# Layer 1's causal masks: from TensorE matmuls to VectorE and GpSimd

## The reference

```
# layer 1's attention; x is the modulated layer norm, 2048 x 128
k = x @ Wk
v = x @ Wv
q = jnp.einsum('btc,qcd->bqtd', x, Wq)
wei = jnp.einsum('bqtd,bsd->bqts', q, k) * scale
causal = jnp.tril(jnp.ones((t, t), dtype=bool))
wei = jnp.where(causal, wei, -jnp.inf)
wei = jax.nn.softmax(wei, axis=-1)
out = jnp.einsum('bqts,bsd->btqd', wei, v)
out = out.reshape(b, t, -1)
return out @ Wp + bp
# around it
h = _layernorm(x, axis=-1) * (1 + ca) + sa
x = x + ga * _L1_attn_ref(h, Wk, Wv, Wq, Wp, bp)
h = _layernorm(x, axis=-1) * (1 + cb) + sb
x = x + gb * _L1_ffn_ref(h, W_r, W_k, W_v, mu_r, mu_k)
```

## Time and profile before

| | us |
|---|---|
| median of three runs | 1150.22 |
| lowest, highest run | 1148.53, 1151.46 |
| profiled execution | 1151.61 |
| its span, first to last instruction | 1149.2 |
| PE busy (matmuls) | 1021.7 |
| DVE busy | 903.9 |
| ACT busy | 814.9 |
| POOL busy | 149.0 |

### The profile page before, as it was taken

How to read it: one execution, slowest core, us unless ns; L and a number is a source line. 1 busy time by engine, 2 the same in 40 slices (tenths; PEclk the granted TensorE clock), 3 DMA queues, 4 the chain that set the end, 5 groups by cost and what they waited for, 6 DMA issues and landing times.

```text
span 1149.2 us, 22131 instructions
## 1 busy us (share of the span) xinstructions
PE 1021.7 (89%) x8766; PEld 349.2 (30%) x8766; DVE 903.9 (79%) x1154; ACT 814.9 (71%) x1556; POOL 149.0 (13%) x264
## 2 busy tenths in 40 slices
PE   4658999999999999999998999899978888798895
PEld 1212222222222222222232444343434443233323
DVE  5897999998999989999988777666766568587602
ACT  3105999998999998999976676567743555466683
POOL 2005000004000013000034000410121003000100
PEclk8658999999999999999999999999989999899997
DMA  4650400002000001000003431052003211200000
GB/s 105 128 98 17 137 2 2 2 2 44 1 2 2 2 21 23 2 1 3 2 2 116 122 87 31 27 93 49 1 1 111 74 57 28 38 10 2 10 1 9
DMA packets 47259, 42.04 MB, mean 37 GB/s; under 512 B 6102, under 2 KB 45366, under 8 KB 47158
## 3 DMA queue, kind: packets, MB, share of 16 engines
q1 hardware_dynamic: 44902, 35.27, 13.2%
q0 software_dynamic: 1824, 5.25, 1.6%
q10 hardware_dynamic: 432, 0.13, 0.0%
HBM read 26.83 MB, written 13.30 MB: 35 GB/s over the span
## 4 chain that ended last, share of the span: by engine, by line
PE 65%; DVE 21%; ACT 7%; issue 3%; DMA 2%; POOL 1%; SPq 1%; POOLq 0%; DVEq 0%; ACTq 0%
PE O L875 23%; DVE mx L1120 13%; PE T L846 12%; PE S L805 7%; PE S L812 4%; ACT PT L1351 3%; PE T L855 3%; PE S L961 2%; PE S L919 1%; PE S L929 1%; PE T L969 1%; PE S L920 1%; PE S L855 1%; PE T L884 1%; DVE Vf L1180 1%
## 5 line engine op out<-in xcount | busy, mean ns | idle before, releaser
L1120 DVE TENSOR_REDUCE mx<-S 128x2 f32<-128x1024 f32 (+2 forms) x672 | 757.0, 1179 | 89.2 <-PE S L812 38.2
L1351 ACT ACTIVATE PT<-T 128x512 f32<-128x512 f32 (+2 forms) x1280 | 675.8, 581 | 118.1 <-PE T L846 46.8
L875 PE MATMUL O<-PT,Va 128*9 128x256 f32 (+1 forms) x4040 | 319.0, 388 | 3.3 <-ACT Os L1358 3.3
L805 PE MATMUL S<-Ks,Qs 48*128 48x512 bf16 x1024 | 208.0, 397 | 26.3 <-DVE mx L1120 22.0
L846 PE MATMUL T<-Qs,Ks 51*128 51x512 bf16 x1024 | 202.1, 387 | 15.3 <-ACT PT L1351 7.2
L846 PEld LDWEIGHTS T<-Qs,Ks 51*128 51x128 bf16 x1024 | 55.6, 93 | 226.4 <-issue 131.9
L875 PEld LDWEIGHTS O<-PT,Va 128*9 128x9 f32 x4040 | 60.0, 88 | 207.4 <-issue 198.0
L812 PE MATMUL S<-K,Qs 96*128 96x512 bf16 (+3 forms) x320 | 85.5, 358 | 15.7 <-DMA Qs<-rows_q 5.4
L855 PE MATMUL T<-Qs,K 99*128 99x512 bf16 (+3 forms) x256 | 72.2, 350 | 7.7 <-ACT PT L1351 4.0
L875 PE MATMUL O<-PT,V 128*17 128x512 f32 (+3 forms) x640 | 75.0, 541 | 0.0
L805 PEld LDWEIGHTS S<-Ks,Qs 48*128 48x128 bf16 x1024 | 52.5, 95 | 53.4 <-DVE mx L1120 47.9
(11 more groups left out here) (225 smaller groups left out, 835.3 us busy)
## 6 DMA issues: line engine op xcount, KB each, us to landing
Qs<-in_L_ffn_experts SPq DMA_DIRECT2D x28, 192.0 KB, 2.7
Ks<-in_L_ffn_experts SPq DMA_DIRECT2D x20, 192.0 KB, 2.6
Qs<-rows_q SPq DMA_DIRECT2D x48, 64.0 KB
Vf<-sorted_x SPq DMA_DIRECT2D x12, 256.0 KB, 4.5
sorted_y<-Vf SPq DMA_DIRECT2D x12, 256.0 KB, 2.3
Qs<-rows_q SPq DMA_DIRECT2D x24, 128.0 KB, 4.6
rows_q<-q SPq DMA_DIRECT2D x7, 384.0 KB, 2.6
sorted_x<-XP POOLq DMA_DIRECT2D x1, 1792.0 KB, 10.8
```

The lines of the kernel that those rows point to most:

```text
L805: m = e.matmul(two[:, i, :], Qs[r0:r0 + 48, hp, q0:q0 + 128], Ks[r0:r0 + 48, hp, CH * kb:CH * kb + CH], start=True, stop=True, tile_positi ...
L875: m = e.matmul(Ob[32 * g:32 * g + d1, lo:hi], v, PT[(2 * j + g // 2) % 4][:, p0 + lo:p0 + hi], start=(kt == 0 and halves[0] == 0), stop=Tr ...
L1120: e.tensor_reduce(mx[:, u % 2, h0:h0 + 2, kb], two[:, :, 0:n], AX.X, ALU.max).then_inc(free, 1)
L1351: e.activation(PT[(2 * j + pair) % 4][:, CH * i + lo:CH * i + CH], bank[:, lo:CH], ACT.Exp).then_inc(free, 1)
```

## The change

The mask matmuls of both passes are gone from PE (256 of them), and so is the tensor `mk`. In the score pass DVE does the work for diagonal tiles: instead of one reduction over both heads it issues a fused operation for each head. It adds `mq`, now 512 columns wide (zeros, and the triangle in the last 128), to the scores, writes the sum back in place to PSUM, and gives the maximum into `mx`. In the exponential pass nothing is masked before the exponential; afterwards POOL sets the entries of `PT` above the diagonal to zero, with one selection for each head pair on 128 by 2 by 128 elements, and signals `masked`. PE's PV waits for that signal in these steps. Tile `bvb` now shares space with `rk`.

```
+        if L == 1 and kt >= 4 * UNITS[1][u][0]:
+            P.masks[L, j, pair] = len(P.masks) + 1
...
# PE, score pass
                             m = e.matmul(two[:, i, 0:n], Q1[0:96, 4 * quad + 2 * pair + i, q0:q0 + 128], K1[0:96, CH * kb:CH * kb + n], start=True, stop=True)
-                            if kb == c:
-                                pe.wait_ge(po_const, PO["mq"])
-                                m = e.matmul(two[:, i, n - 128:n], idb[:, :], mq[:, :], start=False, stop=True, skip_group_check=True)
...
# PE, exponential pass
                             m = e.matmul(bank[:, lo:CH], K1[0:99, keys], Q1[0:99, 4 * quad + 2 * pair + i, CH * c + lo:CH * c + CH], start=True, stop=True)
-                            if kt >= 4 * c:
-                                pe.wait_ge(po_const, PO["mk"])
-                                m = e.matmul(bank[:, lo:lo + 128], idb[:, :], mk[:, :], start=False, stop=True, skip_group_check=True)
...
# PE, pv
                     for g in range(4):
-                        done(("st", L, j, 2 * (g // 2) if (L, j, g // 2) in P.wide else g))
+                        if (L, j, g // 2) in P.masks:
+                            pe.wait_ge(masked, P.masks[L, j, g // 2])
+                        else:
+                            done(("st", L, j, 2 * (g // 2) if (L, j, g // 2) in P.wide else g))
...
# DVE, score pass
+                    if L == 1 and kb == UNITS[1][u][0]:
+                        n = 128 * (qt + 1)
+                        dv.wait_ge(po_const, PO["mq"])
+                        for i in range(2):
+                            m = e.tensor_tensor_reduce(two[:, i, 0:n], two[:, i, 0:n], mq[:, CH - n:CH], 1.0, NEG, ALU.add, ALU.max,
+                                                       mx[:, u % 2, h0 + i, kb:kb + 1])
+                        m.then_inc(free, 1)
+                        continue
...
# POOL
+                elif name == "st" and (a[0], a[1], a[4]) in P.masks:
+                    L, j, u, kt, pair = a
+                    for i in range(2):
+                        done(("st", L, j, 2 * pair if (L, j, pair) in P.wide else 2 * pair + i))
+                    lo = first_col(L, u, kt)
+                    both = PT[(2 * j + pair) % 4][:, :].rearrange("p (i n) -> p i n", i=2)[:, :, lo:lo + 128]
+                    e.affine_select(out=both, in_=both, compare_op=ALU.is_ge, fill=0.0, base=0, pattern=[[0, 2], [1, 128]],
+                                    channel_multiplier=-1).then_inc(masked, 1)
```

More of the change, by code:

```diff
@@ L33 @@
 STEPS0 = 256
-PO = {n: i + 1 for i, n in enumerate(("ones", "k1", "mh", "id0", "id", "h0", "va", "idb", "mq0", "mk0",
-                                      "mq", "mk", "it0", "it1", "ub0", "xp0", "ub"))}
+PO = {n: i + 1 for i, n in enumerate(("ones", "k1", "mh", "id0", "id", "h0", "va", "idb", "mq0", "mq", "it0", "it1", "ub0", "xp0", "ub"))}
 SCALED = {n: i + 1 for i, n in enumerate(("wo", "bo", "bp", "wp", "wvv", "dn"))}
@@ L62, in __init__ @@
         self.slot, self.split_eng, self.xh_prev, self.pv = {}, {}, {}, {}
-        self.wide = set()
+        self.wide, self.masks = set(), {}
         self.xb = self.pvs = self.s_next = self.t_next = 0
@@ L546, in adaln_two_layers @@
         bq, bk, bqs, bv = (sb(n, [128, 1]) for n in ("bq", "bk", "bqs", "bv"))
-        bvb, boB, bpB = (sb(n, [128, 128]) for n in ("bvb", "boB", "bpB"))
+        boB, bpB = (sb(n, [128, 128]) for n in ("boB", "bpB"))
         rwT = sb("rwT", [128, 16])
@@ L578, in adaln_two_layers @@
         rt = sb("rt", [128, 12, 16])
+        bvb = rk[:, 0:128]
         lg, eq, wv_ = (rt[:, 4 * i:4 * i + 4, :] for i in range(3))
@@ L638, in adaln_two_layers @@
         shift_in = [sem(f"shift_in{i}") for i in range(4)]
-        pv_done = sem("pv_done")
+        pv_done, masked = sem("pv_done"), sem("masked")
         zero_x, one_hot, positions, expert_rows, score = (sem(n) for n in ("zero_x", "one_hot", "positions", "expert_rows", "score"))
```

12 lines of the change are left out of this document (4 added, 8 removed).

## The result

The changed kernel takes 1153.41 us (median of 20 runs, 1151.36 to 1160.60) against 1150.65 us for the kernel before in the same comparison (20 runs, 1147.96 to 1155.40). The ratio is 1.0032 with a 95% interval of 1.0018 to 1.0046: some 3.7 us slower, where 2.7 us faster was forecast. The profiled execution of the changed kernel took 1156.31 us, with a span of 1154.3, so it is one of the longer ones.

A forecast was written before the change was run, and what follows sets the result against it. TensorE was taken as the bound at 768 to 840, trading waits with VectorE at 840 to 1000. Gained 10.8 us less 8.1 lost gave 2.7 us faster, from 1150.2 to 1147.5 us; range 1140 to 1158.

The forecast's parts named there:

- The price of a matmul: Mask matmuls on TensorE: 60 ns each by the distance of starts, 15.4 us if all 256 lie on the path.
- 10.8 us gained: TensorE in layer 1's attention, 256 mask matmuls removed: 5.5, 2.6, 1.7 and 1.0 us in the four stretches.
- the masks' places: Share of masks counted as on the path: 92 fully, half of 88, 28 of 40, 16 of 36.
- 23 us forecast: DVE's 64 score tiles: 0.36 us more each, from second starts and accumulator reads, most of it in idle time.
- Rival 2: DVE's fused operation runs at half rate, adding 65 us of DVE work: 17 us slower, 1167; chance 0.10.
- experts' stretch: 840 to 1000 us: 20 DVE tiles add 7.2 us, of which a third, 2.3 us, shows.
- the places: PV delayed by GpSimd's selections: unit 2 1.3 us, chunk 3's normalisation 1.2, units 6 and 7 1.4, tail 0.6.
- The last scatter: POOL's four scatters spread between selections, the last about 10 us later; hidden with 4 us to spare, cost 0.
- The additions: Work added on DVE and GpSimd in layer 1's attention, with PV's wait for selections: 8.1 us lost.
- Rival 3: POOL's queue order costs two to three times the count, sorted rows come late: 7 slower than forecast, 1155; chance 0.20.
- 768 to 840: Sign in TensorE's rows: this stretch gets shorter by about 2 us; more than 4 speaks for PE winning (1141, chance 0.22).
- PV's waits for the selection: Sign in TensorE's waits: the selection named as releaser with 4 to 6 us in all; 10 or more means slower queues.

The follow-up runs named there:

- double: The kernel before with each of its 256 mask matmuls issued twice: ratio 1.0089, 10.2 us slower.
- nomask: The kernel before with its 256 mask matmuls taken away and nothing in their place, diagonal blocks left without causal masks: ratio 0.9999.
- both: The changed kernel with all 256 mask matmuls back on TensorE beside the work of DVE and POOL: ratio 1.0055 to the kernel before.
- dve_part: The kernel before with only the score pass changed, so 128 mask matmuls less and DVE adding the triangle: ratio 0.9999, 1148.9 us.

## Why the prediction was wrong

**The price of a matmul: right.** 60 ns, 10.8 us on the path; double measured 10.2, the fit 9.7.

**The gain as a whole ("10.8 us gained"): wrong, since it has no term for the clock, and this is the step that failed.** The prediction took the price of the masks at full clock and gave it back as a gain, with the clock of the kernel before; that the clock would stay is put in no words and given no reason. What it counted of the masks' places (all 92, half of 88, 28 of 40, 16 of 36) came out about right, 9.7 us (0.8) by the fit above. It read the clock only as a column of the earlier trace rows. The masks are also work that TensorE does, between short matmuls of the diagonal and ahead of its waits; without them the half rate grows from 105 us to 121 and 125, and 128 of them gone give 110. At the 0.47 us of the fit the 20 us of nomask cost 9.4 us, if they lie in the attention, of a gain of 10.8 that is missing; between both and the changed kernel 13 us of it cost 6, where 8.2 are missing. So the clock is most of what is missing, and with the errors of these figures it can be all of it. The cause was tested: removal alone brings 0 (nomask), doubling costs 10.2, and other work in waits brings back 5.3 us without masks and 3.9 in the changed kernel; the 2 beside the masks are not clear of noise. Not shown is why the clock falls more often without the masks at any one place, since single traces of one number of masks differ.

**DVE: 23 us forecast, 9.9 measured in the page, since the read is hidden.** The fused operation runs at full rate, 721 ns for 512 columns, and the read takes 142, as bounded. But the read runs beside the next operation. DVE at unit 6's last masked tiles, against the earlier trace rows:

```profile
1033.00 0.14 DVE L1121 DVE_READ_ACCUMULATOR2_ANT mx<- 128x1 f32 x1
1033.00 0.73 DVE L1121 CUSTOM_DVE_ANT_0 S<-S,mq 128x512 f32<-128x512 f32 x1
1033.65 0.14 DVE L1121 DVE_READ_ACCUMULATOR2_ANT mx<- 128x1 f32 x1
1033.65 0.73 DVE L1121 CUSTOM_DVE_ANT_0 S<-S,mq 128x512 f32<-128x512 f32 x1
...
1035.13 0.22 DVE L1134 TENSOR_REDUCE nm<-mx 128x16 f32<-128x64 f32 x1
```

Read and next operation start together, 0.65 us behind the one before: a tile of two heads takes 1.30 us in a row and 1.40 alone, where the reduction took 1.22 alone and 1.18 in a row. That is 0.1 to 0.2 us for each tile, not 0.36. Rival 2 (half rate) didn't happen.

In the experts' stretch, where the forecast was 2.3 us, TensorE waits 2.1 us more for maxima. That the two numbers agree is luck: the 2.3 are a third of 7.2 us of added work, DVE's busy time there grew by 2.0 us, and 1.1 of the 2.1 us are in nomask as well.

**GpSimd: the places were right.** A selection takes 0.41 us (0.45 forecast), and the handover to TensorE is 0.05 us (834.56 + 0.40 to 835.01), not 0.15. PV waited 0.79 us at unit 2 (1.3 forecast), 1.93 at the normalisation, less the 1.07 which TensorE waited there before, so 0.9 (1.2), 0.90 and 0.48 at units 6 and 7 (1.4 for both), 0.2 at 885 us, and 1.2 us in the tail in four pieces (0.6). Together 4.4 us against 4.5. The last scatter came 10.5 us later (877.26 against 866.80 in the earlier trace rows) and the sorted rows still in time: their first use is at 890.17, against the earlier trace rows.

**The sum.** The additions were forecast at 8.1 us and measured at 6.3 (both). The gain was forecast at 10.8, and 2.6 of it are there. The sign was lost in the second number alone. The additions were too high by DVE's part (3.6 forecast, 1.6 by the fit), not by GpSimd's (4.5 and 4.0). Rival 3 gave 1155 and the time was near it, but not for its reason: the sorted rows were not late and the queue cost what the forecast said.

**The signs named in advance.** 768 to 840 did not get shorter by 2 us: at unit 0's turn the changed kernel is 0.5 us ahead, at unit 1's 0.3 behind. PV's waits for the selection are 5.5 us in all, 4 to 6 as forecast. None of the signs looked at the clock, so none could have shown the fault.

## What to carry to other kernels

In this kernel work removed from TensorE was a gain only as far as the clock stayed. Before counting such a gain, look at the granted clock of the stretches and at the waits behind which it falls, and price the removal by an experiment that puts nothing in its place. Adding the same work a second time tells whether it lies on the path, and a few useless matmuls in a wait tell what the clock is worth there. A new handover on a nearly idle engine can cost little by itself: 55 of the 64 selections here held nobody up. It cost where the selection stood behind something in that engine's queue, and in the tail.

## What the runs showed of the hardware

- Taking 256 matmuls of 128 columns away from 1150 us raised TensorE's time at the half rate by 16 to 20 us, and the time did not fall; 32 matmuls of 512 columns in three waits lowered it by 10 to 17 us (each kernel taken against the kernel before of its comparison) and the time by 2 to 5 us in three kernels, and by 1 us each in a fourth (dve_part), which is no change that these runs can tell.
- One us at the half rate is not one price. In the attention of layer 1, where TensorE is the bound or near it, it costs 0.47 us by the fit to 14 traces. Over the whole execution the time of the kernel before rises by only 0.15 us for each us at the half rate from run to run (31 runs of the first comparison); much of what varies there lies in the first 115 us.
- DVE's addition with a maximum, in place in PSUM with a bf16 operand in SBUF, takes 721, 587, 452 and 318 ns for 512, 384, 256 and 128 columns, about 1.05 ns for each further column, like a plain maximum (687 and 1217 ns for 512 and 1024); its accumulator read of 142 ns starts with the next operation and costs only behind the last.
- GpSimd's selection over 128x2x128 takes 412 ns, in line with 287 for 128 columns.
